# Cross attention by chunks: softmax and weighted sums half a chunk behind the projections, first and last step rewritten

## What is computed

```python
def proj(x, W, b):
    y = jnp.einsum('btd,ed->bte', x, W) + b
    return y.reshape(B, -1, H, DK).transpose(0, 2, 1, 3)
q = proj(Q, Wq, bq); k = proj(K, Wk, bk); v = proj(V, Wv, bv)
scores = jnp.einsum('bhqd,bhkd->bhqk', q, k) / jnp.sqrt(jnp.float32(DK))
attn = jax.nn.softmax(scores, axis=-1)
out = jnp.einsum('bhqk,bhkd->bhqd', attn, v)
...
x = x + _L0_xattn_ref(_layernorm(x, axis=-1), ctx_1024, ctx_1024, ...)
x = x + _L0_attn_ref(_layernorm(x, axis=-1), ...)    # self attention with a bias by distance
x = x + _L0_ffn_ref(_layernorm(x, axis=-1), ...)     # 8 experts, the best 2 weighted
```

## Time and profile before

| | us |
|---|---|
| median of 3 runs | 1583.5 (1582.37 to 1584.36) |
| the profiled execution | 1580.36 |
| its span, first to last instruction | 1578.6 |
| PE busy | 1518.5 (96%) |
| DVE busy | 1311.8 (83%) |
| ACT busy | 1266.7 (80%) |
| POOL busy | 939.6 (60%) |
| chain that ended last: PE | 88% |
| the same: DVE | 5% |

### The profile page before, as it was taken

How to read it: one execution, slowest core, us unless ns; L and a number is a source line. 1 busy time by engine, 2 the same in 40 slices (tenths; PEclk the granted TensorE clock), 3 DMA queues, 4 the chain that set the end, 5 groups by cost and what they waited for, 6 DMA issues and landing times.

```text
span 1578.6 us, 48054 instructions
## 1 busy us (share of the span) xinstructions
PE 1518.5 (96%) x17880; PEld 1254.2 (79%) x17880; DVE 1311.8 (83%) x1759; ACT 1266.7 (80%) x3054; POOL 939.6 (60%) x948
## 2 busy tenths in 40 slices
PE   6999999999999999999999999999999677999998
PEld 5788888888888888888888888888877555777776
DVE  7788888888888888888888888988888876767665
ACT  4888888888888888888888888888888765655554
POOL 5668787787877878778787787877866231000000
PEclk9999999999999999999999999999999787999999
DMA  4366655656566565665655656556565877655550
GB/s 180 75 137 115 138 115 135 139 114 136 114 137 139 113 137 114 135 140 113 139 113 133 144 109 140 120 125 146 108 135 110 171 174 238 216 203 197 209 203 25
DMA packets 460019, 220.24 MB, mean 140 GB/s; under 512 B 433840, under 2 KB 439984, under 8 KB 453184
## 3 DMA queue, kind: packets, MB, share of 16 engines
q1 hardware_dynamic: 459536, 218.22, 57.8%
q10 hardware_dynamic: 432, 1.32, 0.3%
HBM read 111.96 MB, written 0.56 MB: 71 GB/s over the span
## 4 chain that ended last, share of the span: by engine, by line
PE 88%; DVE 5%; DMA 2%; ACT 2%; POOL 1%; issue 1%; SPq 0%; POOLq 0%; DVEq 0%; ACTq 0%
PE ps_proj L1318 53%; PE ps_proj L1540 10%; PE ps_s L1368 9%; PE ps_o L1386 8%; PE ps_o L1563 5%; DMA pt_s<-p_s 2%; PE ps_proj L1347 1%; POOL ctx_s L421 1%; DVE cmax L948 1%; DVE wsp L1161 1%; DVE p_s L961 1%; DMA ctx_f<-ctxt_dram 1%; ACT prob L623 0%; PE ps_o L1288 0%; PE ps_o L1463 0%
## 5 line engine op out<-in xcount | busy, mean ns | idle before, releaser
L1318 PE MATMUL ps_proj<-ctx_s,wk_s 128*128 128x256 f16 x4032 | 480.6, 273 | 3.9 <-ACT ps_proj L577 3.6
L1318 PE MATMUL ps_proj<-wv_s,ctx_s 128*128 128x256 f16 x4032 | 480.6, 273 | 1.5 <-ACT ps_proj L579 1.5
L1318 PEld LDWEIGHTS ps_proj<-ctx_s,wk_s 128*128 128x128 f16 x4032 | 380.0, 98 | 66.4 <-issue 24.3
L421 POOL TENSOR_TENSOR ctx_s<-t_f,ctx_s 128x512 f16<-128x512 f32 x192 | 266.3, 1398 | 279.2 <-ACT ctx_s L525 279.2
L1318 PEld LDWEIGHTS ps_proj<-wv_s,ctx_s 128*128 128x128 f16 x4032 | 379.9, 98 | 63.5 <-issue 11.2
L623 ACT ACTIVATE prob<-ps_s,nmax 128x256 f32<-128x256 f32 x776 | 357.0, 476 | 8.0 <-DVE nmax L955 7.8
L948 DVE TENSOR_REDUCE cmax<-ps_s 128x4 f32<-128x1024 f32 x194 | 237.5, 1224 | 123.4 <-PE ps_s L1368 123.3
L961 DVE SCALAR_TENSOR_TENSOR p_s<-prob,p_s 128x1024 f16<-128x1024 f32 x196 | 321.2, 1639 | 0.7 <-ACT p_s L634 0.7
L421 POOL TENSOR_TENSOR ctx_s<-ctx_f,ctx_s 128x512 f16<-128x512 f32 x144 | 216.1, 1501 | 9.7 <-ACT ctx_s L520 4.8
L634 ACT ACTIVATE p_s<-prob 128x1024 f16<-128x1024 f32 x196 | 206.7, 1054 | 6.7
L1386 PE MATMUL ps_o<-v_s,pt_s 128*128 128x64 f16 x4704 | 172.2, 194 | 14.0 <-DMA pt_s<-p_s 14.0
(11 more groups left out here) (178 smaller groups left out, 1781.9 us busy)
## 6 DMA issues: line engine op xcount, KB each, us to landing
ctx_f<-ctxt_dram SPq DMA_DIRECT2D x48, 1024.0 KB, 5.5
wst<-w_dram SPq DMA_DIRECT2D x96, 512.0 KB, 4.7
pt_s<-p_s SPq DMA_TRANSPOSE x408, 3.1
tisa<-tisa_scores SPq DMA_DIRECT2D x12, 256.0 KB, 5.7
w_in_f<-w_in_dram SPq DMA_DIRECT2D x2, 1024.0 KB, 6.0
w_f<-wk_dram SPq DMA_DIRECT2D x2, 512.0 KB, 6.2
ctx_f<-ctxt_dram SPq DMA_DIRECT2D x2, 512.0 KB, 7.7
w_f<-wv_dram SPq DMA_DIRECT2D x1, 1024.0 KB, 11.3
```

What stands on the lines that cost most here:

```text
L421: pool.tensor_tensor(out=low[:, n, :, :], in0=sources[n], in1=high[:, n, :, :], op=ALU.subtract).then_inc(ctx_low, 1)
L1318: ins = pe.matmul(ps_proj[:, bank(h, role), sub * QUARTER:(sub + 1) * QUARTER], lhsT, rhs, start=(fresh and sub == 0 and t == 0 and i == 0 ...
```

## The change

**Steps.** For step c >= 0 the half h now works on k = c+h and g = 2(1-h)+half. The K half does scores(c, 2), weigh(c, 0), scores(c, 3), weigh(c, 1); the V half does scores(c+1, 0), weigh(c, 2), scores(c+1, 1), weigh(c, 3). The lag of two groups stays. So the V half multiplies with the K blocks whose units ran in the K half just ahead, and `scores` waits for `block_low` at 8k+3 (C11, C22, C12) for g = 0, and at 8k+4 for g = 2. Maxima, exponentials, p_highs and p_lows go along. `alphas`, `add_o`, `rescale` and `step_max` swap their halves, and SP's transposes move by two slots. `cross_steps` ends a step earlier. The blocks leave the banks in the order in which they left them before.

**First step.** PE, ACT and DVE get a `first_step`: K's four plain groups, the queries, V's first two, scores(0, 0), V's last two, scores(0, 1). DVE does K's lows, the queries, K's weight sum lows, two V lows, the maxima of (0, 0), two V lows, V's weight sum lows, the maxima of (0, 1), bias_rows and p_lows(0, 0).

**Last step.** Two scores are left in it (`ps_proj` for g = 2, `ps_s` for g = 3) and four weighs; DVE's list is shorter by two maxima, one `add_o` and two p_lows.

```diff
         def score_bank(c, g, head):
-            return ps_proj[:, head, :] if isinstance(c, int) and c == LAST and g % 2 else ps_s[:, head, :]
+            return ps_proj[:, head, :] if in_proj(c, g) else ps_s[:, head, :]    # in_proj: (LAST, 2)
...
             def scores(c, g, odd):
-                if g == 0:
-                    pe.wait_ge(block_low, 8 * c + 4)
+                if g % 2 == 0:
+                    pe.wait_ge(block_low, 8 * c + 3 + g // 2)
...
                     for half, before, between, behind in ((0, (M1,), (M5, M6), (M2,)), (1, (), (M7, M3), (M4,))):
-                        g = 2 * h + half
+                        k, g = c + h, 2 * (1 - h) + half
                         units(*before)
-                        if exists(c, 0):
-                            scores(c, g, odd)
+                        scores(k, g, odd if h == 0 else 1 - odd)
                         units(*between)
-                        vc, vg = back(c, g, PV_LAG)
-                        if exists(vc, 0):
-                            weigh(vc, vg, odd if g >= PV_LAG else 1 - odd)
+                        vc, vg = back(k, g, PV_LAG)
+                        weigh(vc, vg, odd)
                         units(*behind)
...
+            def first_step():                       # PE
+                for g in range(NG):
+                    if g == 2:
+                        turn(0)
+                    plain(0, g)
+                project_q()
+                for half in range(2):
+                    plain(1, 2 * half)
+                    plain(1, 2 * half + 1)
+                    scores(0, half, 0)
...
             def last_step():                        # DVE
                 block_lows(LAST, 1, C21, LAST % 2)
-                maxima(LAST, 0, LAST % 2)
-                p_lows(LAST - 1, 3)
-                maxima(LAST, 1, LAST % 2)
-                add_o(LAST - 1, 0)
-                tisa_scores()
-                p_lows(LAST, 0)
-                add_o(LAST - 1, 1)
                 maxima(LAST, 2, LAST % 2)
                 p_lows(LAST, 1)
                 maxima(LAST, 3, LAST % 2)
+                add_o(LAST - 1, 1)
+                tisa_scores()
+                p_lows(LAST, 2)
                 last_base(0)
-                p_lows(LAST, 2)
                 p_lows(LAST, 3)
```

More of the change, by code:

```diff
@@ L280, in cross_steps @@
                 step(r + 1, 1)
-            for c in range(LOOP_END, NCH + 1):
+            for c in range(LOOP_END, NCH):
                 step(c, c % 2)
@@ L321, in step @@
             def step(c, odd):
-                for g in range(NG):
-                    if exists(c, 0):
-                        turn_p(c, g)
-                    if g == 0 and exists(c, 3) and after(c, 0):
+                for slot in range(NG):
+                    if exists(c, slot // 2) and after(c, slot // 2):
+                        turn_p(c + slot // 2, (slot + 2) % NG)
+                    if slot == 0 and exists(c, 3) and after(c, 0):
                         sp.wait_ge(ctx_low, UNITS * (c + 2))
@@ L683, in step @@
                         act.activation(tisa_e[:, h, :], tisa_e[:, h, :], ACT.Exp).then_inc(tisa_exp, 1)
+            def first_step():
+                for g in range(NG):
+                    plain_highs(0, g)
+                weight_sum_highs(0)
+                for half in range(2):
+                    ctx_highs(1, 1, half)
+                weight_sum_highs(1)
+                for g in range(2):
+                    plain_highs(1, g)
+                exps(0, 0, 0)
+                p_highs(0, 0)
+                for g in range(2, NG):
+                    plain_highs(1, g)
+                exps(0, 1, 0)
             for half in range(2):
@@ L692, in _ @@
                 weight_high(1, half)
-            cross_steps(act, step)
+            cross_steps(act, lambda c, odd: step(c, odd) if after(c, 0) else first_step())
             act.wait_ge(unit_done, units_through(2 * NCH))
@@ L1046, in step @@
                         block_lows(c + h, 1 - h, C21, odd if h == 0 else 1 - odd)
-                    if not after(c, 0):
-                        for g in range(NG):
-                            plain_lows(h, g)
-                        if h == 0:
-                            split_q()
-                            bias_rows()
-                        weight_sum_lows(h)
-                    if exists(c, 0):
-                        maxima(c, 2 * h, odd)
-                    pc, pg = back(c, 2 * h, 1)
+                    k, g, k_odd = c + h, 2 * (1 - h), odd if h == 0 else 1 - odd
+                    if exists(k, 0):
+                        maxima(k, g, k_odd)
+                    pc, pg = back(k, g, 1)
                     if exists(pc, 0):
@@ L1076, in step, with first_step @@
                         w_in_lows(K, h)
+            def first_step():
+                for g in range(NG):
+                    plain_lows(0, g)
+                split_q()
+                weight_sum_lows(0)
+                for g in range(2):
+                    plain_lows(1, g)
+                maxima(0, 0, 0)
+                for g in range(2, NG):
+                    plain_lows(1, g)
+                weight_sum_lows(1)
+                maxima(0, 1, 0)
+                bias_rows()
+                p_lows(0, 0)
             def last_step():
                 block_lows(LAST, 1, C21, LAST % 2)
-                maxima(LAST, 0, LAST % 2)
-                p_lows(LAST - 1, 3)
-                maxima(LAST, 1, LAST % 2)
-                add_o(LAST - 1, 0)
-                tisa_scores()
-                p_lows(LAST, 0)
-                add_o(LAST - 1, 1)
                 maxima(LAST, 2, LAST % 2)
@@ L1392, in step @@
                 for h in range(2):
-                    if not after(c, 0):
-                        for g in range(NG):
-                            if h == 0 and g == 2:
-                                turn(0)
-                            plain(h, g)
-                        if h == 0:
-                            project_q()
                     def units(*which):
                         for m in which:
-                            if exists(c, 1) and after(c, 0):
-                                unit(c + 1, 1 - odd, h, m)
+                            unit(c + 1, 1 - odd, h, m)
```

75 lines of the change are left out of this document (35 added, 40 removed).

## The result

The changed kernel takes 1595.26 us (1593.86 to 1596.04, 4 runs), the kernel before 1583.93 (1582.37 to 1584.84, 4 runs): 1.0072 times as long, 95% interval 1.0056 to 1.0088. It is slower by 11.3 us; 1589.8 was forecast, with 1595.5 as the upper end. The profiled execution took 1593.86, with a span of 1592.1, 13.5 more than the 1578.6 of before.

What follows compares the result with a forecast made beforehand. PE was taken to bound the kernel, all matmuls in the loop. Start +9.0, loop wait +4.7, step 46 +0.7 and last step -8.1 gave +6.3: 1583.5 + 6.3 = 1589.8 us, range 1584.0 to 1595.5.

Steps and rivals of the forecast that it cites:

- The stall at the start: PE idle ahead of scores(0, 2) while DVE's queue delays maxima(0, 1): 6.3 us, the greatest stall of the change.
- the wait in the loop: V half's first scores wait for C12's low: 0.11 us per chunk over 43 chunks, +4.7 us (0 to 5.6).
- the shorter last step: After the last projections two softmax groups are left, not four, with DVE as the chain: -8.1 us (-7.5 to -9.5).
- The term of step 46: Where DVE and ACT also do the bias table, C12's lows end late and scores wait: +0.7 us (0.5 to 1.0).
- the fallen clock: Rival, chance 0.17: idle time at the start drops PE's clock to 1.2 GHz, giving 1591 to 1595 us.
- What bounds the kernel: PE, busy in 200.00 of 200 us of the steady loop; only new stalls or the two ends can change the time.
- The rival that a wait met 0.09 us ahead is free: Loop, chance 0.15: the sequencer's wait costs nothing with 0.09 us of margin; +1.6 in all, 1585.1 us.
- the estimate of 0.04 us of stall from the lower end: Loop: with a semaphore read of 0.05 us in place of 0.12, the stall is 0.04 us, in all 1.7.
- The start: First step up to the V half's scores of step 1, with DVE and POOL clashing: +9.0 us (+4.6 to +10.5).
- half a chunk and a chunk: From scores(0, 2) to step 1's V-half scores: 12.3 + 24.6 us, plus 1.45 and 1.0 for late transposes.
- The queries' cast: Start: if only two SBUF inputs made DVE clash with POOL, this cast would not wait; the start would cost 8.4.
- Sum: All terms together: +6.3 us on the median of 1583.5, that is 1589.8 us.

Runs made afterwards that it cites:

- e1: The kernel before with one wait added: the V half's first scores also wait for C12's low of the next chunk; 1584.68 us, before 1583.92.
- e2: The changed kernel with 24 matmuls of unused result in PE's 6.3 us of idle time ahead of scores(0, 2); 1589.0 us.
- e3: The changed kernel with ACT's two exponentials of the bias table one step later, in step 46 and not 45; 1588.34 us.
- e7: The kernel before with DVE's and ACT's bias table work spread over the V halves of steps 45 to 47; 1577.27 us, ratio 0.9969.
- e9: The changed kernel with ACT's K-half context highs behind the C12 highs and POOL's rescale and step_max ahead of its context lows there; 1586.59 us.
- e6: The changed kernel with DVE's first step reordered: maxima(0, 0) and (0, 1) ahead of K's and V's weight sums, bias_rows between; 1589.24 us.
- e11: The changed kernel with the edits of e9 and e10 together; 1575.58 us, ratio 0.9958 to the kernel before.
- e4: The changed kernel with ACT's K-half context highs behind the exponentials of the second group, no longer ahead of them; 1658.95 us.
- e5: The changed kernel with ACT's K-half context highs behind the C22 and C12 highs, POOL's order unchanged; 1769.76 us.
- e10: The changed kernel with e6 and e7, and V's weight sums moved behind maxima(0, 2); 1580.58 us, ratio 0.9989 to the kernel before.
- e8: The changed kernel with the edits of e5, e6 and e7 together; 1764.12 us.

## Why the prediction was right in sign and half of the size

The stall at the start, the wait in the loop and the shorter last step came as described. The term of step 46 stood for 0.7 us and the steps around it cost 5.2, by another mechanism, and a rival that had been priced separately, the fallen clock, came true as well. That 1595.26 lies in the range, 0.2 us below its upper end, is in part luck: the clock rival had set that end, and much of the way up to it was made by the bias table, for which neither a term nor a rival stood.

- **What bounds the kernel**: right. PE was the bound in the loop, and all changes came from new stalls and from the two ends.
- **The wait in the loop**, +4.7 forecast: right in mechanism, a little too large. It is 0.094 us a chunk over the 39 chunks from 6 to 45, 3.7 in all. e1 splits it into 0.05 for the wait and 0.04 for later data, where I had 0.03 and 0.08. The rival that a wait met 0.09 us ahead is free is refuted by e1. DVE's low ended at 618.15 and the scores started at 618.28, so this row says 0.13 from release to start. The Trainium skill gives 50 to 100 ns for reading a semaphore ("Advanced Engine Details and Errata", section "Network/Comms"). The row lies above that, and the estimate of 0.04 us of stall from the lower end was too small.
- **The start**, +9.0 forecast: the layout held nearly to the row (q_s lows end at 40.31, forecast 39.8; K's sums 43.54, forecast 43.1; maxima(0, 1) with nmax 54.53, forecast 54.1; scores(0, 2) 56.64, forecast 56.1, with the stall of 6.3). What failed is the step behind it, "half a chunk and a chunk" with 1.45 and 1.0 us for late transposes: weigh(0, 0) waited for nothing (at 61.96), and one transpose of 0.45 (at 81.36) was all. In their place the clock was not full, and PE lost 0.6 and 1.3 us in the two rows at 1.2 GHz, and the scores at 71.86 waited 0.93 for C12's low. It also let the orders settle at once, where chunks 3 to 5 still had two waits for C12's low (0.31 and 0.34 us) and two for transposes (0.59 and 0.52). At chunk 2's V half the scores stand at 97.37, 10.9 behind before and not 9.0; at chunk 6 the offset is 12.25.
- **The queries' cast**: it took 1.17 us beside POOL and 0.69 in before, though it has one SBUF input. So the two-input part alone, which I weighed at 8.4 for the start, doesn't describe it. The Trainium skill says that an operation in a two-port mode contends too ("SBUF — State Buffer", section "Who interferes with whom"); this row agrees.
- **Step 46**, +0.7 forecast, 5.2 for the steps around it: the term that failed. I read one row, C12's two lows at 1200.09, and costed the new wait on it. In the profiled execution that wait cost nothing (the scores at 1221.56 come 1.40 us after their M1), though it was there in e2 (0.46 us) and e1 (0.89). I did not follow what else stood in the two halves before: ACT waits 4.33 and 3.65 us in them for DVE's arguments with a seed queued behind (4.35 and 3.56 before). How long PE stands for it depends, as I read the rows, on how far ACT and DVE are ahead of PE when it begins. In before PE had just waited 1.00 us for a transpose, and C12's low ended 0.13 us behind the start of that V half (1170.27 to 1170.14); in after it ended 1.55 behind it (1188.26 to 1186.71). To this the clock adds 0.7 + 0.6 + 0.4 us (2.17, 1.49 and 1.86 against 1.48, 0.86 and 1.47), after an idle time of 2.74 us. e3 and e7 show the queue to be behind the stalls: with it gone, so are the stalls at the seeds and the fall of the clock. How much it costs is not a fixed number: the same stretch took 79.75 us in before, 81.8 in e1, 81.7 in e2, 82.2 in e9, 84.6 in e6 and 85.0 in after. So 5.2 is what two executions give, and e2 against before gives 1.9.
- **The last step**, -8.1 forecast: from the scores on it is 1276.61 - 1258.98 = 17.6 us against 1262.58 - 1236.71 = 25.9, that is 8.2 less. From the V half's first matmul on it is 7.1 less, since the first scores of that step wait 0.59 us for a V low (`block_low` at 8 LAST + 7) and a weigh before them 0.42. DVE's list set the end, as laid out; from the last p_low to its weigh it took 3.8 us (1270.63 to 1274.40) and not the 5.5 of before.
- **Sum**: 12.25 + 3.7 + 5.2 - 7.1 - 0.5 = 13.5 in the profiled executions, 11.3 in the medians. Of the 7 us by which the sum of 6.3 fell short, about 3.6 are the clock at two places (1.9 and 1.7), and with the first of them gone, 1.1 us came back as a wait in e2. The 2.2 us between the two sums are not placed: before's profiled execution is 3.6 us below its median, after's 1.4.

What stays open: e2, e3 and e6 are single times, and the first unit of chunk 1 begins up to 1.8 us apart where the lists up to it are the same (47.02 in e3, 47.74 in e2, 48.85 in after). I used distances within one timeline for that reason. The shorter last step was not tried without the new start and loop. POOL's order of e9 was not tried without ACT's. What decides whether the clock falls after an idle time of 2 to 3 us is open.

## What to carry to other kernels

A rare piece of work (a table, a last load) that is put into a tight loop at one place is paid where an in-order engine waits for it with something urgent queued behind; look for that queue before moving anything, since a shift of the loop by fractions of a microsecond changes what it costs. Spread over idle time it left no stall at the seeds: e7 is 0.3% faster for 20 lines. Test such a mend in the kernel before as well: here it gave 4.7 us there, and without e7 the gain of e11 would have been put down to the change. A wait that is met just in time is not free (0.05 us a chunk here), and the remedy for data that come 0.1 us late may need the orders of two engines changed together (e9), when one of them alone costs 64 or 175 us (e4, e5).

## What the runs showed of the hardware

- PE's granted clock fell to 1.2 GHz behind idle times as short as 1.99 us (e9), 2.00 (e1), 2.16 (e11) and 2.24 (e6). It held behind 2.04 (e2), 2.16 (e10), 2.17 (e6), 2.26 (before), 2.48 (e9) 2.71 in some chunks of e5 and 3.10 in e8. So between 2.0 and 3.1 us the length of the idle time does not decide it. Behind 6.3 us it fell in each trace that has such a stall (after, e3, e4, e9). A fall cost PE 1.4 to 2.3 us of matmul time. Matmuls in the gap of 6.3 us held the clock up (e2).
- A DVE operation that shares its time with POOL takes longer by amounts that vary: p_low takes 1.22 us, or 1.37 to 2.38 (both in e9), the pair of weight sums 2.35, 3.31 or 4.50.
